# Page loop of a routed expert layer: VectorE's combination one page later, transposes three pages ahead, other ring sizes

## The reference

```
logits = xn @ Wr + br                      # 8192 tokens, 8 experts
top_vals, top_idx = top_k(logits, 2);  w = softmax(top_vals)
for e in range(8):
    h = gelu(xn @ W1[e] + b1[e])           # 128 -> 256
    y += (h @ W2[e] + b2[e]) * w_full[..., e, None]
x = x + y
```

## Time and profile before

| | |
|---|---|
| median of 3 runs | 870.4 us (867.45 to 872.46) |
| the profiled execution's own time | 872.07 us |
| its span, first to last instruction | 870.3 us |
| PE busy | 688.5 us, 79% |
| DVE busy | 618.9 us, 71% |
| ACT busy | 431.9 us, 50% |
| POOL busy | 309.5 us, 36% |
| first matmul of page 0 to first matmul of page 90 | 681.09 to 854.11 us, 173.02 us |

### The profile page before, as it was taken

The page is one execution under the profiler, slowest core; times in us unless marked ns, Lnnn a source line. Parts: engine busy times, 40 slices in busy tenths (PEclk is TensorE's granted clock), DMA queues, the critical chain, the costliest instruction groups (busy, mean ns, idle before and its releaser), DMA issues.

```text
span 870.3 us, 23444 instructions
## 1 busy us (share of the span) xinstructions
PE 688.5 (79%) x7545; PEld 493.1 (57%) x7545; DVE 618.9 (71%) x3004; ACT 431.9 (50%) x1572; POOL 309.5 (36%) x486
## 2 busy tenths in 40 slices
PE   0995898888878787878888888888683899878994
PEld 0774665554445454545454545676561688777883
DVE  5334777777777777777777777486575488777894
ACT  1113565444444445454545454253432588777883
POOL 4700112322232222222121212357677255445553
PEclk9997655555555555555555555798896899999997
DMA  5993111101111111111111110544322333333330
GB/s 132 163 228 113 32 43 32 44 31 43 30 42 31 42 31 43 30 42 30 42 31 43 35 43 18 181 143 154 120 89 102 85 97 106 92 94 95 104 96 7
DMA packets 75403, 64.38 MB, mean 74 GB/s; under 512 B 8344, under 2 KB 72189, under 8 KB 75309
## 3 DMA queue, kind: packets, MB, share of 16 engines
q1 hardware_dynamic: 67715, 50.31, 22.1%
q0 software_dynamic: 5984, 12.74, 4.0%
q10 hardware_dynamic: 1636, 0.48, 0.2%
HBM read 37.94 MB, written 27.32 MB: 75 GB/s over the span
## 4 chain that ended last, share of the span: by engine, by line
PE 37%; DVE 30%; ACT 17%; issue 12%; POOL 1%; another core or an unknown queue 0%; DMA 0%; DVEq 0%; POOLq 0%; SPq 0%; ACTq 0%
PE pb L811 10%; DVE pb L1460 8%; ACT tanh_c L1130 5%; DVE h L1462 5%; ACT GC L1126 4%; ACT S L1128 3%; PE pb L1029 3%; PE pb L848 2%; PE pb L1012 2%; DVE glo L1633 2%; PE pb L1014 2%; PE pb L875 2%; ACT adjT L1145 2%; PE pb L725 2%; PE pb L1013 1%
## 5 line engine op out<-in xcount | busy, mean ns | idle before, releaser
L811 PEld LDWEIGHTS pb<-h,vp 128*128 128x128 bf16 x3840 | 142.3, 106 | 190.8 <-DVE h L1462 187.8
L811 PE MATMUL pb<-h,vp 128*128 128x32 f16 x3840 | 171.3, 190 | 54.8 <-DVE h L1462 41.4
L689 POOL DMA_INDIRECT out<-outb,out_i x91 | 91.0, 999 | 95.6 <-DVE outb L1645 70.0
L780 PE MATMUL pb<-xbuf,us 128*128 128x256 f32 x198 | 117.5, 699 | 0.0
L1126 ACT ACTIVATE GC<-pb 128x32 f32<-128x32 f32 x256 | 51.2, 200 | 129.8 <-PE pb L811 129.8
L1460 DVE TENSOR_TENSOR_SCAN pb<-S,GC 128x64 f32<-128x64 f32 x256 | 77.4, 302 | 32.2 <-ACT S L1128 18.5
L1130 ACT ACTIVATE tanh_c<-pb 128x32 f32<-128x32 f32 x256 | 50.6, 198 | 96.1 <-DVE pb L1460 96.1
L1462 DVE SCALAR_TENSOR_TENSOR h<-S,tanh_c 128x32 f16<-128x32 f32 x256 | 49.3, 192 | 67.5 <-ACT tanh_c L1130 67.5
L1012 PE MATMUL pb<-xT,w 128*128 128x128 f16 x364 | 66.4, 221 | 23.2 <-DVE xT L1627 18.3
L1236 ACT ACTIVATE Gl<-pb,pw 128x512 f32<-128x512 f32 x91 | 62.5, 687 | 26.8 <-PE pb L1014 23.4
L1633 DVE SCALAR_TENSOR_TENSOR glo<-Gl,pw,ghi 128x512 f16<-128x512 f32 x91 | 68.1, 749 | 9.4 <-ACT ghi L1242 6.0
(11 more groups left out here) (331 smaller groups left out, 1629.1 us busy)
## 6 DMA issues: line engine op xcount, KB each, us to landing
Xp<-xs_d SPq DMA_DIRECT2D x91, 130.0 KB
adjn<-in_adj SPq DMA_DIRECT2D x32, 256.0 KB, 2.7
x_d<-x2s SPq DMA_DIRECT2D x33, 128.0 KB, 1.8
y_d<-ys SPq DMA_DIRECT2D x33, 128.0 KB, 1.8
X<-in_x SPq DMA_DIRECT2D x4, 912.0 KB, 18.5
xs_d<-zrow SPq DMA_DIRECT2D x1, 3640.0 KB, 13.9
yr<-y_d SPq DMA_DIRECT2D x8, 256.0 KB
x2r<-x_d SPq DMA_DIRECT2D x8, 256.0 KB
```

Source lines behind the costliest of these rows:

```text
L689: pool.indirect_dma_start(out_rows, bass.IndirectOffsetOnAxis(out_i[t % NOUT][:, 0:1], 0), outb[t % NOUT][:], None, bounds_check=B * T - 1 ...
L780: mm(o, us[:, q, :], xbuf[:], start=False, stop=False, skip_group_check=True)
L811: return mm(o, vp[p][:, q, :], h[:], start=False, stop=True, skip_group_check=True)
```

## The change

In the page loop the combination in DVE's order moves one page later, so an iteration is combine(t-3), gelu_lower(t), page_lower(t+3); in the last iteration both combine(t-3) and combine(t-2) stand ahead of gelu_lower. PE's transpose and ACT's and DVE's copies of the tile move from two to three pages ahead; layer1 and layer2 keep their places. The transpose gets one wait more, for `page_lower` of the page two before it, whose PSUM bank it writes again. The ring `Xp` goes from seven to ten buffers; their loads share four semaphores in turn, and a load waits until the one four before it has landed. The rings `outb` and `out_i` go from eight to four. A few semaphores of the set-up are split or renamed, with each wait on the same event as before.

```diff
-NOUT = 8
 NLD = 4
-XR = 7
+XR = 10
+NXL = 4
...
-        outb, out_i = ring("outb", NOUT, [P, D]), ring("out_i", NOUT, [P, 1], U32)
+        outb, out_i = ring("outb", 4, [P, D]), ring("out_i", 4, [P, 1], U32)
...
                 if t >= XR:
                     sp.wait_ge(out_ready, t - XR + 1)
-                sp.dma_start(Xp[t % XR][:], xs_d[bass.ds(rows[t % ROWS], P), :]).then_inc(page_loaded[t % XR], 16)
+                if t >= NXL:
+                    sp.wait_ge(page_loaded[t % NXL], 16 * (t // NXL))
+                sp.dma_start(Xp[t % XR][:], xs_d[bass.ds(rows[t % ROWS], P), :]).then_inc(page_loaded[t % NXL], 16)
...
             def page_transpose(t):
-                pe.wait_ge(page_loaded[t % XR], 16 * (t // XR + 1))
+                pe.wait_ge(page_loaded[t % NXL], 16 * (t // NXL + 1))
+                if t >= 2:
+                    pe.wait_ge(xl_ready, t - 1)
                 tr(PT[t % 2], Xp[t % XR][:, P:2 * P], ident).then_inc(xt_ps, 1)
...
                 layer1(t)
                 if t >= 2:
                     layer2(t - 2)
-                if t + 2 < PAGES:
-                    page_transpose(t + 2)
+                if t == 0:
+                    page_transpose(2)
+                if t + 3 < PAGES:
+                    page_transpose(t + 3)
                 if t + 1 < PAGES:
                     addresses(t + 1)
...
                 gelu(t)
                 gelu_upper(t)
-                if t + 2 < PAGES:
-                    page_evacuate(t + 2)
+                if t == 0:
+                    page_evacuate(2)
+                if t + 3 < PAGES:
+                    page_evacuate(t + 3)
...
                 dve.wait_ge(l2_ps, t + 1)
-                if t >= NOUT:
-                    dve.wait_ge(out_stored[t % NOUT], 16 * (t // NOUT))
+                if t >= 4:
+                    dve.wait_ge(out_stored[t % 4], 16 * (t // 4))
...
             for t in range(PAGES):
-                if t >= 2:
+                if t >= 3:
+                    combine(t - 3)
+                if t == PAGES - 1:
                     combine(t - 2)
                 gelu_lower(t)
-                if t + 2 < PAGES:
-                    page_lower(t + 2)
+                if t == 0:
+                    page_lower(2)
+                if t + 3 < PAGES:
+                    page_lower(t + 3)
```

More of the change, by code:

```diff
@@ L317, in build @@
         rows_sent = [sem(f"rows_sent{i}") for i in range(NBUF)]
-        page_loaded = [sem(f"page_loaded{i}") for i in range(XR)]
+        page_loaded = [sem(f"page_loaded{i}") for i in range(NXL)]
         y_loaded = [sem(f"y_loaded{i}") for i in range(NLD)]
         x2_loaded = [sem(f"x2_loaded{i}") for i in range(NLD)]
-        out_stored = [sem(f"out_stored{i}") for i in range(NOUT)]
+        out_stored = [sem(f"out_stored{i}") for i in range(4)]
         tok = lambda a: a.rearrange("b (i s) d -> s b i d", s=TT)
@@ L447, in _ @@
                     sp.wait_ge(out_ready, t - XR + 1)
-                sp.dma_start(Xp[t % XR][:], xs_d[bass.ds(rows[t % ROWS], P), :]).then_inc(page_loaded[t % XR], 16)
-            for i in range(NOUT):
-                sp.wait_ge(out_stored[i], 16 * len(range(i, PAGES, NOUT)))
+                if t >= NXL:
+                    sp.wait_ge(page_loaded[t % NXL], 16 * (t // NXL))
+                sp.dma_start(Xp[t % XR][:], xs_d[bass.ds(rows[t % ROWS], P), :]).then_inc(page_loaded[t % NXL], 16)
+            for i in range(4):
+                sp.wait_ge(out_stored[i], 16 * len(range(i, PAGES, 4)))
         @block.gpsimd
@@ L513, in _ @@
             tp.memset(folded[:], 0.0)
-            tp.tensor_copy(onesh[:], ones).then_inc(setup_ready, 1)
+            tp.tensor_copy(onesh[:], ones).then_inc(prep_ready, 1)
             pool.wait_ge(gwT_sb, 1)
@@ L688, in _ @@
                 pool.wait_ge(out_ready, t + 1)
-                pool.indirect_dma_start(out_rows, bass.IndirectOffsetOnAxis(out_i[t % NOUT][:, 0:1], 0), outb[t % NOUT][:], None,
-                                        bounds_check=B * T - 1, oob_is_err=False).then_inc(out_stored[t % NOUT], 16)
+                pool.indirect_dma_start(out_rows, bass.IndirectOffsetOnAxis(out_i[t % 4][:, 0:1], 0), outb[t % 4][:], None,
+                                        bounds_check=B * T - 1, oob_is_err=False).then_inc(out_stored[t % 4], 16)
         @block.tensor
@@ L1074, in _ @@
             act.wait_ge(dgs_ready, 1)
-            av(dgr[:], dgs[:], ACT.Sqrt).then_inc(roots_exps, 1)
+            av(dgr[:], dgs[:], ACT.Sqrt).then_inc(dgr_ready, 1)
             act.wait_ge(exp_in, 1)
-            av(fe[:], fw[:], ACT.Exp, bias=fmax[:, 0:1], accum_out=fs[:]).then_inc(roots_exps, 1)
+            av(fe[:], fw[:], ACT.Exp, bias=fmax[:, 0:1], accum_out=fs[:]).then_inc(exp_out, 1)
             for c in range(4):
@@ L1271, in _ @@
                 ins = v.bn_aggr(mv_a[:, i, :], st_a[:, i, :])
-            ins.then_inc(var_ready, 1)
-            dve.wait_ge(rstd_ready, 1)
+            ins.then_inc(var_a, 1)
+            dve.wait_ge(rstd_a, 1)
             for i in range(NTILE):
@@ L1639, in combine @@
                 dve.wait_ge(l2_ps, t + 1)
-                if t >= NOUT:
-                    dve.wait_ge(out_stored[t % NOUT], 16 * (t // NOUT))
+                if t >= 4:
+                    dve.wait_ge(out_stored[t % 4], 16 * (t // 4))
                 ins = v.scalar_tensor_tensor(out=ra[t % 2][:], in0=y[:, 0:P], scalar=x[:, 2 * P:2 * P + 1], in1=x[:, 0:P], op0=ALU.mult, op1=ALU.add)
-                v.tensor_scalar(out_i[t % NOUT][:], x[:, 2 * P + 2:2 * P + 3], valid[:, t:t + 1], float(SKIP), ALU.mult, ALU.add)
+                v.tensor_scalar(out_i[t % 4][:], x[:, 2 * P + 2:2 * P + 3], valid[:, t:t + 1], float(SKIP), ALU.mult, ALU.add)
                 link(ins)
-                v.scalar_tensor_tensor(out=outb[t % NOUT][:], in0=y[:, P:2 * P], scalar=x[:, 2 * P + 1:2 * P + 2], in1=ra[t % 2][:], op0=ALU.mult, op1=ALU.add).then_inc(out_ready, 1)
+                v.scalar_tensor_tensor(out=outb[t % 4][:], in0=y[:, P:2 * P], scalar=x[:, 2 * P + 1:2 * P + 2], in1=ra[t % 2][:], op0=ALU.mult, op1=ALU.add).then_inc(out_ready, 1)
             page_lower(0)
```

32 lines of the change are left out of this document (16 added, 16 removed).

## The result

| | before | after |
|---|---|---|
| median of 20 runs | 873.86 us (867.45 to 882.40) | 884.14 us (871.99 to 893.10) |
| profiled execution, its span | 872.07, 870.3 us | 893.10, 891.3 us |
| start of the loop | 681.09 | 687.20 us |
| loop, page 0's to page 90's first matmul | 173.02 | 185.43 us |
| from there to the end | 16.2 | 18.7 us |

The account below looks back on a forecast made before the run. The prediction took a two-page chain across PE, ACT and DVE as the bound, then PE's work: 90 x 1.69 = 152.1, plus 2.2 interruption and 0.5 start, 154.8 against 173.0 us, so 852.2 us, range 847 to 859 (chance 0.68).

Parts of the forecast that it names:

- The bound after the change: Page loop: PE's own work bounds it at 1.66 us a page, taken as 1.69 with 0.03 for jitter.
- The 2.2 us of an interruption: Loop, 785.93 to 791.77 us: two pages 2.2 us over the good rate, cause unnamed, kept in the forecast.
- I take the chain as complete: Good stretch of the loop before: 3.43 us chain for two pages plus 0.08 register load gives the measured 1.80 a page.
- Even a signal 1.1 us late leaves it ended at 1.8: DVE: the later combination, even with layer2's signal 1.1 us late, ends at 1.8, before gelu_lower can start at 2.42.
- the 0.83 us to spare ahead of layer2: Head of layer2 on PE: gelu_lower ends at 3.17, layer2 follows at 4.00, so 0.83 us are spare.
- no change: Rival: signals late on every page make layer2 wait 0.27 us, 1.96 a page; 870 us; chance 0.08.
- Half of it: Rival: signals 1.1 us late on every second page, 1.82 a page; 6.5 us less, 863.9 us; chance 0.17.
- Four output buffers: Rival: combine(t) waits for page t-4's store; at 7.5 us a store, 2.04 a page and 883.7 us; chance 0.06.
- POOL blocked by DVE: Rival: POOL can't work during gelu_lower's 0.75 us, so 2.25 us a page and 902 us; chance 0.01.
- The transpose's wait: PE, ahead of page_transpose(t+3): extra wait for page_lower(t+1), claimed to cost nothing with 1.4 us margin.
- The SP loads and ten buffers: Row loads on SP, four in flight: a load every 0.7 us at most against 1.69 needed; claimed to cost nothing.
- The combination's move: DVE order: combine(t-3) reads what layer2 finished an iteration earlier, done while DVE waits for ACT's copy, hiding late signals.

Follow-up runs that it names:

- again: The changed kernel itself, run again unaltered beside the kernel before, no late signals: 843.85 against 847.22 us, ratio 0.9961, loop 150.57 us.
- again2: The changed kernel unaltered, run again beside the kernel before on another chip, no late signals: ratio 0.9958, loop 151.90 us.
- again3: The changed kernel unaltered, run again beside the kernel before, no late signals: ratio 0.9955, loop 151.75 us.
- before_again: The kernel before, unchanged, run against itself for a new trace, no late signals: ratio 1.001, loop 156.17 us.
- paced2: Changed kernel with layer1(t) waiting for page t+1's copy and no separate transpose wait, a few late signals: 0.9901 of the kernel before, loop 162.31 us.
- again4: The changed kernel unaltered, run again beside the kernel before, with late signals: 882.54 against 872.02 us, ratio 1.0117, loop 184.83 us.
- split2: Changed kernel without the transpose's extra wait, register load right behind layer1, with late signals: 1.0178 of the kernel before, loop 186.16 us.
- late_after: Changed kernel with layer1's signal given 0.61 us later, by a matmul of layer2(t-2); natural late signals too: 0.9918 of the kernel before, loop 177.28 us.
- late_before: Kernel before with layer1's signal given 0.61 us later, by a matmul of layer2(t-2): 0.9895 of the unedited kernel before, loop 179.84 us.
- split: Changed kernel without the transpose's extra wait, register load between layer1 and layer2, with late signals: 0.996 of the kernel before, loop 185.78 us.
- nowait: Changed kernel without the transpose's extra wait, its event covered by layer2's wait, no late signals: 0.9942 of the kernel before, loop 149.96 us.
- comb: Kernel before with only the combination moved one page later, seven row buffers, no late signals: 1.0234 of the kernel before, loop 172.80 us.
- tr3: Changed kernel with the combination back at two pages behind, the rest kept, no late signals: 0.9955 of the kernel before, loop 151.76 us.
- comb10: Kernel before with the combination one page later, ten row buffers and four load signals, no late signals: 0.9987 of the kernel before, loop 153.78 us.
- paced: Changed kernel with layer1(t) waiting for page t+1's copy and no separate transpose wait, no late signals: 1.0022 of the kernel before, loop 155.49 us.

## Why the prediction was wrong

**The bound after the change was right, and shown where signals are punctual.** 154.8 us were forecast for the loop; `again`, `again2` and `again3` took 150.6 to 151.9, 1.67 to 1.69 a page (150.57 / 90, 151.90 / 90) against 1.69. PE is the bound, most of the idle time that is left stands behind the register load (5.3 of 7.0 us in `again`), and DVE's wait for layer2 is gone (it was idle ahead of `ra` for 0.4 us). The 2.2 us of an interruption did not come back.

**The first step that failed: "I take the chain as complete", and that the 173 us were the chain.** The register load was added to it, 1.715 + 0.08 = 1.80, and that the sum met the stretch's rate was luck. In `before_again` the load makes two pages 0.10 us longer once in four pages, 0.03 a page: most of it lies in a pause in which PE waits for the chain in any case. What filled the good stretch were late signals. From 814.80 to 850.74 layer1's are recorded 0.01 to 0.39 us behind their rows, 0.19 on average, and each enters the chain of two pages once, 0.09 a page. The chain alone makes 154.4 us of loop and the kernel before takes 155.5 to 156.2 without late signals; the other 17 us of the earlier trace rows are missing wherever signals are punctual. The sum credited the change with all of them, though it takes only the combination's share of them out of the chain. What it takes from the true loop is 4.3 us in the second set and 3.7 in the fourth, and with 1.2 us more after the loop (17.36 against 16.16 us from page 90 to the end) 2.5 to 3.1 us are left; the medians say 3.1 to 3.8, or 0.4%, under the bound that the prediction set for a change.

**The second, which set the sign: "Even a signal 1.1 us late leaves it ended at 1.8".** It took 1.1 us for the size of lateness, and for the same before and after. The trace of before already had one of 2.51 us, with a pause of PE inside a block beside it, and the prediction kept that stretch as an interruption "in no chain that I can name". After the change the signals that were late were later, at least 1.36 us on average against 0.63, up to 3.4 us, past the 0.83 us to spare ahead of layer2. So the idle time at the heads of blocks that the change was to take away stayed (22.6 us, 22.5 before), and the pauses inside blocks, of which the prediction has no term, came on top: steps of 14.2 us in all against 0.5, which covers the 12.4 us by which the loop grew. The rival "no change" had this mechanism and this place (wait moved to the head of layer2: 6.0 us at L1027) and was priced with 1.1 us of lateness; it got 0.08. The prediction's last sentence named the condition (signals late on every page, or interruptions that grow), and no chance of its own stood behind it. That lateness grows where the order leaves PE fewer waits is what `paced2`, `again4` and `split2` say: same set, same work, 162, 185 and 186 us. It is not shown beyond them, since in the third set `late_after` had late signals with nearly as much idle time of PE as `late_before`, and `split` was no slower than the kernel before. What it is in the order that makes the difference stays open.

**The rivals.** *Half of it* assumed 1.1 us on every second page and fell: it still expected a gain. *Four output buffers*: not it, though its 883.7 us is next to the 884.14 measured, by coincidence. `again` runs with four of them at 1.67 a page, and DVE was idle ahead of `ra` for 0.4 us in all, there as in the result's trace. *POOL blocked by DVE*: fell, as the trace of before already had it; most of POOL's idle time is named for the combination (76.0 us, 34 times, in the result's trace).

**The parts costed at nothing.** The transpose's wait: some 0.2% by `nowait`, near the noise but not clearly nothing. The SP loads and ten buffers: nothing, and necessary, since the later combination with seven costs 2.3% (`comb`). The combination's move, to which the prediction gave the hiding of late signals: without late ones it is worth nothing (`tr3` 0.9955, `again` 0.9961), with ten buffers and nothing else 0.13% (`comb10`, an interval that includes 1). What it is worth with late ones wasn't measured, as `tr3` and `comb10` ran only where signals were punctual.

The Trainium skill (Perfetto Trace Analysis, the part on the Tensor Engine instruction) says that the end of a matmul in the profile is computed from its size and that the signal comes after it. The runs agree in kind: an idle engine started 0.04 us after the computed end in sets 1, 2 and 4, and up to 3.8 us after it (in `split`) in the others.

**What stays open.** Why signals are late in the result's runs and in sets 3 and 5 and not in the others. Programs and data are the same, and the kernel before shows it too (847 us against 872 to 894), so it is not the change; the chip differs from set to set, and no two sets share one, so a property of the chip and one of the moment can't be told apart. The granted clock doesn't differ (0.99 to 1.00 in the loop). Nor does the supply of instructions, as far as the traces tell: 34 packets of them in the loop, with a median of 0.94 us in the result's trace and 0.93 in `again`. Whether PE really ran late, or only its signals, can't be read, as the rows' ends are computed. Why `paced2` has few late signals wasn't found. Whether the changed kernel would absorb 1.1 us of lateness on a chip without any wasn't measured, since `late_after` met natural lateness. The best version depends on it too: `nowait` where signals are punctual (0.9942), `paced` on the one chip with late ones where it ran (0.9901, and 1.0022 otherwise).

## What to carry to other kernels

Before the gap between a chain and the measured rate is credited to a change, find out what it is: here an execution of the *unchanged* kernel on another chip, at 156 instead of 173 us, would have shown that 17 us weren't the program's. A stretch that is slow for no reason that can be named deserves the same look as the rest; here it was the mechanism that decided. Compare the start of a waiting engine with the end of the row it waited for; if the two lie over 0.3 us apart at some pages, price a rival in which that grows, because in the result and in the fifth set taking PE's regular waits away cost more than the waits did. And when a reader of a buffer moves later, count the ring that it frees: one page later with seven buffers cost 2.3%, with ten nothing.

## What the runs showed of the hardware

- The same program has a loop of 151 to 152 us in three sets, and of 185 in the fifth set and in the result, at a granted clock of 0.99 to 1.00 in all of them. The timed runs say the same as the traces, 844 and 883 us (and 884 in the result). The kernel before moves less between them, 847 to 872 (and 894 in one set). Not all of it is in the loop: that starts at 672 to 675 us in sets 1, 2 and 4 and at 681 to 687 in the others.
- An idle engine started 0.04 us after the end of the matmul's row, wherever one waited, in sets 1, 2 and 4, and up to 3.8 us after it in the others. Only PE's signals are late there: the recorded ones of ACT and DVE stand within 0.02 us of their rows' ends in every trace. In the result's trace, in `again4`, `split` and `split2` PE's own matmuls also pause for 0.3 to 0.5 us in the middle of a block for nothing that the profile names, 8.3 us in all in the changed kernel and 16.7 in `split`.
- A kernel whose PE waits for a later event on every page was 22 us faster in its loop than the one that doesn't (`paced2`, `again4`, one chip).
- A register load from SBUF on PE takes 0.78 us for three registers and 0.85 for twelve.
